# Causal attention with two heads' scores in PSUM: each head's probabilities turned into the banks of its own scores

## The reference, cut to what matters

```python
q_word, k_word, v_word = jnp.split(word_hidden_states @ c_attn_w + c_attn_b, 3, axis=-1)
k = concatenate([k_img, k_word]); v = concatenate([v_img, v_word])     # one image token first
scores = einsum('bhqd,bhkd->bhqk', q, k) / sqrt(8)
scores = where(kj <= qi + 1, scores, -10000.0) + mask
out = einsum('bhqk,bhkd->bhqd', softmax(scores), v)
```

## Time and profile before

| | |
|---|---|
| median of 3 executions | 843.94 us (838.22 to 846.42) |
| profiled execution, its own time | 842.1 us |
| its span in the profile | 839.5 us |
| stage C, from the first score matmul to the last transpose back | 362.8 to 504.4 us of the span |
| PE, DVE, ACT busy over the whole span | 80%, 73%, 62% |

### The profile page before, as it was taken

The page is one execution under the profiler, slowest core; times in us unless marked ns, Lnnn a source line. Parts: engine busy times, 40 slices in busy tenths (PEclk is TensorE's granted clock), DMA queues, the critical chain, the costliest instruction groups (busy, mean ns, idle before and its releaser), DMA issues.

```text
span 839.5 us, 12933 instructions
## 1 busy us (share of the span) xinstructions
PE 670.8 (80%) x4514; PEld 400.6 (48%) x4514; DVE 616.5 (73%) x1349; ACT 520.1 (62%) x1237; POOL 169.6 (20%) x169
## 2 busy tenths in 40 slices
PE   7589976777889889679987878577888695779866
PEld 3222231543556556445555545254656543446545
DVE  7882348468999897777777765999676669986864
ACT  4479977654778778145775764645665475565742
POOL 5030040012889789711000000000000000000000
PEclk8879987887555555956999998879999897899998
DMA  9400000000000000000000000000000000000000
GB/s 300 140 1 1 2 2 0 1 0 1 1 2 1 1 2 1 1 0 1 2 1 1 2 2 0 1 0 1 2 2 1 1 0 1 0 2 1 1 1 25
DMA packets 9059, 10.54 MB, mean 13 GB/s; under 512 B 2746, under 2 KB 7844, under 8 KB 8868
## 3 DMA queue, kind: packets, MB, share of 16 engines
q1 hardware_dynamic: 8996, 9.73, 3.6%
HBM read 9.21 MB, written 0.52 MB: 12 GB/s over the span
## 4 chain that ended last, share of the span: by engine, by line
PE 43%; DVE 36%; ACT 11%; issue 9%; POOL 1%; DMA 0%; ACTq 0%; DVEq 0%; POOLq 0%
PE ps L1390 4%; PE ps L1650 4%; PE ps L1553 4%; DVE s_nmB L1032 3%; DVE s_nmD L1311 3%; PE ps L1633 3%; ACT arena L514 2%; PE ps L1737 2%; PE ps L1540 2%; PE ps L1670 2%; PE ps L1461 2%; PE ps L1745 2%; PE ps L1831 2%; PE ps L1433 2%; PE ps L1812 2%
## 5 line engine op out<-in xcount | busy, mean ns | idle before, releaser
L382 POOL TENSOR_SCALAR arena<-arena,s_rB,s_zpu 128x512 uint8<-128x512 f32 x128 | 115.9, 945 | 42.5 <-DVE s_rB L1005 41.2
L552 ACT ACTIVATE arena<-ps,s_nmB 128x512 f32<-128x512 f32 x128 | 86.6, 683 | 31.8 <-DVE s_nmB L1032 31.2
L574 ACT ACTIVATE arena<-ps,s_nmx 128x512 f32<-128x512 f32 (+3 forms) x128 | 60.7, 527 | 50.2 <-DVE s_nmx L1130 49.7
L1032 DVE TENSOR_REDUCE s_nmB<-ps 128x2 f32<-128x1024 f32 x64 | 77.3, 1217 | 6.9 <-PE ps L1540 6.6
L1125 DVE TENSOR_REDUCE s_nmx<-ps 128x1 f32<-128x512 f32 (+3 forms) x128 | 56.6, 484 | 21.4 <-PE ps L1636 20.9
L514 ACT ACTIVATE arena<-ps 128x1024 f32<-128x1024 f32 x64 | 60.9, 1026 | 6.4 <-PE ps L1445 6.4
L1553 PE MATMUL ps<-cst,arena 128*128 128x128 f32 x256 | 61.0, 417 | 1.7 <-POOL arena L382 0.8
L1396 PE MATMUL ps<-ones 128*128 128x512 f16 x134 | 43.9, 491 | 22.7 <-ACT s_wn L485 6.6
L1540 PE MATMUL ps<-staged 8*128 8x512 f16 x128 | 46.7, 585 | 11.7 <-ACT arena L552 10.9
L1553 PEld LDWEIGHTS ps<-cst,arena 128*128 128x128 f32 x256 | 48.7, 218 | 14.7 <-POOL arena L382 8.2
L1650 PE MATMUL ps<-cst,arena 128*128 128x128 f32 x320 | 46.9, 301 | 8.7 <-issue 5.3
(11 more groups left out here) (344 smaller groups left out, 1515.3 us busy)
## 6 DMA issues: line engine op xcount, KB each, us to landing
vec<-in_vec SPq DMA_DIRECT2D x1, 1882.0 KB, 11.7
w_d<-in_wqkv SPq DMA_DIRECT2D x2, 768.0 KB
vec<-in_vec SPq DMA_DIRECT2D x1, 960.0 KB, 8.2
w_h<-in_w SPq DMA_DIRECT2D x2, 341.0 KB
x_tok<-in_x SPq DMA_DIRECT2D x1, 512.0 KB, 4.1
arena<-in_w_f SPq DMA_DIRECT2D x2, 256.0 KB, 8.0
rope<-in_rope SPq DMA_DIRECT2D x1, 512.0 KB, 10.5
w_do<-in_wo SPq DMA_DIRECT2D x2, 256.0 KB
```

Of the source, the lines that this page charges most:

```text
L382: nc.gpsimd.tensor_scalar(u8[:, n % 4, j // 2, :, 2 * (j % 2)], prob[:, n % 2, j * 512:j * 512 + 512], sm("rB", 8)[:, c:c + 1], sm("zpu", ...
L552: nc.scalar.activation(prob[:, n % 2, j * 512:j * 512 + 512], ps[:, j, :], ACT.Exp, bias=sm("nmB", 8)[:, c:c + 1], accum_out=sm("sumB", 8) ...
L574: nc.scalar.activation(probC[:, n % 2, at(qt):at(qt) + w], ps[:, bank, col:col + w], ACT.Exp, bias=nmx[:, TB * b + qt, h:h + 1]).then_inc( ...
L1032: free(V.tensor_reduce(sm("nmB", 8)[:, c:c + 2], ps[:, 2 * half:2 * half + 2, :], X, ALU.max, negate=True), "maxB")
```

## The change

The separate banks 3 to 5 for the turned probabilities are gone. Head n has its scores in banks 0 to 2 where n is even and in banks 3 to 5 where n is odd (`bank_c`), and its probabilities are turned into the same three banks, once the exponentials of the head have all been taken. Banks 6 and 7 keep their use. With that:

- PE's loop is now: `t_c` of head n; all scores of head n + 2; at odd n `group_c` (the `group_T` of heads n + 3 and n + 4); at n = 4, 8, ... `pv_c`; at n = 6, 10, ... `turn_back`. The scores of head n + 2 wait, bank by bank, for the copies of head n: bank 0 and bank 1 for ACT's, bank 2 for DVE's. `t_c` waits only for the exponentials. The scores of the first two heads are computed ahead of the loop.
- ACT copies the turned banks as two instructions of 512 columns, and they stand between the exponential of tile 3 and those of tiles 2, 0, 1 of the next head. Before, the copy stood behind all four.
- DVE's `stage_c` moves from ahead of the copy L1148 to behind it.
- `ptC` and `ptC_A` count three and two signals per head in place of two and one.

```diff
+        def bank_c(n, bank):
+            return 3 * (n % 2) + bank
...
             for n in range(B * H + 1):
-                b, h = divmod(n, H)
                 if n < B * H:
-                    for i, qt in enumerate((3, 2, 0, 1)):
-                        if i < 2:
-                            act.wait_ge(sem["maxC"], 2 * n + i + 1)
-                        if n >= 2 and i == 0:
-                            act.wait_ge(sem["ptC"], 2 * (n - 1))
...
+                    act.wait_ge(sem["maxC"], 2 * n + 1)
+                    if n >= 2:
+                        act.wait_ge(sem["ptC"], 3 * (n - 1))
+                    exp_c(n, 3)
                 if n >= 1:
                     m = n - 1
-                    act.wait_ge(sem["ptC"], 2 * m + 1)
...
-                    nc.scalar.activation(prob_t(m), ps[:, 3:5, :].rearrange("p a b -> p (a b)"), ACT.Copy).then_inc(sem["ptC_A"], 1)
+                    for i in range(2):
+                        act.wait_ge(sem["ptC"], 3 * m + i + 1)
+                        nc.scalar.activation(prob_t(m)[:, 512 * i:512 * i + 512], ps[:, bank_c(m, i), :], ACT.Copy)\
+                            .then_inc(sem["ptC_A"], 1)
+                if n < B * H:
+                    act.wait_ge(sem["maxC"], 2 * n + 2)
+                    for qt in (2, 0, 1):
+                        exp_c(n, qt)
...
-                    if n % 2 == 0 and n + 2 < B * H:
-                        stage_c(n // 2 + 1)
...
-                    free(V.tensor_copy(prob_v(m), ps[:, 5, 0:256]), "ptC_V")
+                    free(V.tensor_copy(prob_v(m), ps[:, bank_c(m, 2), 0:256]), "ptC_V")
+                if n % 2 == 0 and n + 2 < B * H:
+                    stage_c(n // 2 + 1)
...
-            def s_c(n, parts):
+            def s_c(n, tiles):
...
-                    if n >= 1 and qt:
-                        pe.wait_ge(sem["expC"], 4 * (n - 1) + read)
+                    if n >= 2:
+                        pe.wait_ge(sem["ptC_V" if bank == 2 else "ptC_A"], n - 1 if bank == 2 else 2 * (n - 2) + bank + 1)
...
             def t_c(n):
                 pe.wait_ge(sem["expC"], 4 * n + 4)
-                if n >= 1:
-                    pe.wait_ge(sem["ptC_A"], n)
-                    pe.wait_ge(sem["ptC_V"], n)
...
-                        ins = nc.tensor.transpose(ps[:, 3 + bank, c:c + P], probC[:, n % 2, a:a + P], ident)
-                    if kt in (3, 2):
+                        ins = nc.tensor.transpose(ps[:, bank_c(n, bank), c:c + P], probC[:, n % 2, a:a + P], ident)
+                    if kt != 1:
...
+            group_c(0)
+            for n in range(2):
+                s_c(n, (3,))
+                s_c(n, (2, 0, 1))
+            group_c(1)
+            for n in range(B * H + 3):
                 if n < B * H:
-                    s_c(n, slice(1, 4))
...
+                    t_c(n)
+                if n + 2 < B * H:
+                    s_c(n + 2, (3,))
+                    s_c(n + 2, (2, 0, 1))
+                if n % 2 == 1 and n + 3 < B * H:
+                    if n >= 7 and n % 4 == 3:
+                        pe.wait_ge(sem["oC"], (n - 3) // 4)
+                    group_c((n + 3) // 2)
+                if n >= 4 and n % 4 == 0:
+                    pv_c((n - 4) // 4)
+                if n >= 6 and n % 4 == 2:
+                    g = (n - 6) // 4
                     pe.wait_ge(sem["oT_C"], g + 1)
-                    if n // 2 + 1 <= B * H // 2:
-                        pe.wait_ge(sem["stagedC"], n // 2 + 1)
                     turn_back(7, oT[:, g % 2, :], "toC")
```

More of the change, by code:

```diff
@@ L563, in _, with exp_c @@
             again_c(act, 0, lambda o, a: nc.scalar.activation(o, a, ACT.Copy))
+            def exp_c(n, qt):
+                b, h = divmod(n, H)
+                bank, col = place(qt)
+                w = P * (qt + 1)
+                nc.scalar.activation(probC[:, n % 2, at(qt):at(qt) + w], ps[:, bank_c(n, bank), col:col + w], ACT.Exp,
+                                     bias=nmx[:, TB * b + qt, h:h + 1]).then_inc(sem["expC"], 1)
             for n in range(B * H + 1):
-                b, h = divmod(n, H)
                 if n < B * H:
-                    for i, qt in enumerate((3, 2, 0, 1)):
-                        if i < 2:
-                            act.wait_ge(sem["maxC"], 2 * n + i + 1)
-                        if n >= 2 and i == 0:
-                            act.wait_ge(sem["ptC"], 2 * (n - 1))
[L572 to L575, removed]
+                    act.wait_ge(sem["maxC"], 2 * n + 1)
+                    if n >= 2:
+                        act.wait_ge(sem["ptC"], 3 * (n - 1))
+                    exp_c(n, 3)
                 if n >= 1:
                     m = n - 1
-                    act.wait_ge(sem["ptC"], 2 * m + 1)
                     if m >= 6:
@@ L1124, in _ @@
                             bank, col = place(qt)
-                            ins = V.tensor_reduce(nmx[:, TB * b + qt, h:h + 1], ps[:, bank, col:col + P * (qt + 1)], X,
-                                                  ALU.max, negate=True)
+                            ins = V.tensor_reduce(nmx[:, TB * b + qt, h:h + 1],
+                                                  ps[:, bank_c(n, bank), col:col + P * (qt + 1)], X, ALU.max, negate=True)
                             if qt == tiles[-1]:
@@ L1142, in _ @@
                     m = n - 1
-                    dve.wait_ge(sem["ptC"], 2 * m + 2)
+                    dve.wait_ge(sem["ptC"], 3 * m + 3)
                     if m == 0:
@@ L1626, in s_c @@
                 r = slice(64 * j, 64 * j + 51)
-                for qt, read in ((3, 1), (2, 3), (0, 3), (1, 4))[parts]:
-                    if n >= 1 and qt:
-                        pe.wait_ge(sem["expC"], 4 * (n - 1) + read)
+                for qt in tiles:
                     bank, col = place(qt)
+                    if n >= 2:
+                        pe.wait_ge(sem["ptC_V" if bank == 2 else "ptC_A"], n - 1 if bank == 2 else 2 * (n - 2) + bank + 1)
                     w = P * (qt + 1)
-                    o = ps[:, bank, col:col + w]
-                    M(o, stb[r, G % 2, qt * P:qt * P + P], stb[r, G % 2, 512:512 + w], start=(qt > 0), stop=False)
-                for qt in (3, 2, 0, 1)[parts]:
+                    M(ps[:, bank_c(n, bank), col:col + w], stb[r, G % 2, qt * P:qt * P + P], stb[r, G % 2, 512:512 + w],
+                      start=(qt > 0), stop=False)
+                for qt in tiles:
                     bank, col = place(qt)
-                    ins = M(ps[:, bank, col + P * qt:col + P * qt + P], identb[:, :], cmask[:, :], start=False, stop=(qt != 2))
+                    ins = M(ps[:, bank_c(n, bank), col + P * qt:col + P * qt + P], identb[:, :], cmask[:, :],
+                            start=False, stop=(qt != 2))
                 ins.then_inc(sem["sC"], 1)
@@ L1658, in pv_c @@
                     pe.wait_ge(sem["vC"], b + 1)
-                pe.wait_ge(sem["ptC_A"], 4 * g + 4)
+                pe.wait_ge(sem["ptC_A"], 8 * g + 8)
                 pe.wait_ge(sem["ptC_V"], 4 * g + 4)
@@ L1672, in pv_c, with group_c @@
                 ins.then_inc(sem["pvC"], 1)
-            group_T(0, 7, padqC, padkC, 8, "tC", identb[:, :], psb16)
-            s_c(0, slice(0, 1))
-            for n in range(B * H + 4):
-                if n < B * H:
-                    s_c(n, slice(1, 4))
[L1679 to L1690, removed]
+            def group_c(G):
+                if G == H // 2:
+                    parts_c(1)
+                group_T(G, 7, padqC, padkC, 8, "tC", identb[:, :], psb16)
+            group_c(0)
[4 more added lines that the diff above has]
+            for n in range(B * H + 3):
+                if n < B * H:
+                    t_c(n)
[10 more added lines that the diff above has]
+                    g = (n - 6) // 4
                     pe.wait_ge(sem["oT_C"], g + 1)
-                    if n // 2 + 1 <= B * H // 2:
-                        pe.wait_ge(sem["stagedC"], n // 2 + 1)
                     turn_back(7, oT[:, g % 2, :], "toC")
-                if n >= 5 and n % 4 == 1:
-                    pv_c((n - 5) // 4)
             pe.wait_ge(sem["ocn"], B)
```

## The result

The changed kernel takes 883.12 us (median of 4 executions, 882.13 to 883.53) against 845.18 us for the kernel before on the same chip: a ratio of 1.0453, 95% interval 1.0417 to 1.0488. It is slower by about 38 us. The profiled execution took 882.13 us and its span is 880.3.

A forecast was written before the change was run, and what follows sets the result against it. The prediction took PE, 88% busy in the stage, to set the pace. To 842.1 us it added 26 for waits (six cycles 21, start 5) and 22 for the clock: 890, or 892 on the median, range 862 to 908.

The forecast's parts named there:

- The ring: Stage C: PE's last instruction before the transposes releases, through DVE and ACT, its next scores; PE waits 1.8, 2.4, 1.5 us.
- The three ways round: From group_T through DVE and ACT to PE's scores 3.50 us, with copy L1171 between 4.1, from turn_back 3.2.
- The sum per four heads: Four heads of stage C take 18.8 us against 15.26, 3.5 more; over six cycles +21 us.
- The start of the stage: Ahead of the first pv_c: two more score blocks at clock 0.50 and part of the waits, +5 us, bounds 2.9 and 8.
- The join and the end: Join of the two batches and end of stage C: taken at nothing, bounds -2 and +2 us.
- The clock: Stage C: idle time drops PE's clock to 0.50 in most cycles; 4.4 us in five of seven, +22, bounds none and +34.
- with two pairs 3.8, with three 4.9 us: Cost of a low-clock cycle, by how many pairs of scores and group_T or turn_back (1.15 us each) run slow.
- The swing of the clock: Skill page's rule: cycling through PSUM banks swings the clock; a fall in every cycle, upper bound +34 us, about 902.
- PE was not freed: Rival, 5%: two bank sets give enough slack, PE's 12% of gaps in stage C close, -12 us, 830 to 832.
- The clock did rise in the stage: Rival, 5%, claimed the opposite: the clock never rises in stage C, 80 us more, about 922.
- The rule on repeating gaps: Skill page's rule: gaps repeating on the engine that should be full can mean too few buffers; favoured PE freed, 830 to 832.

The follow-up runs named there:

- e1: The changed kernel with group_c moved ahead of the scores of head n + 2, turn_back left in place; 849.94 us, ratio to before 1.0106.
- e3: The changed kernel with both group_c and turn_back moved ahead of the scores of head n + 2; 843.68 us, ratio to before 0.9981.
- e4: The changed kernel with ACT's two copies of head n ahead of the tile 3 exponential of head n + 1; 862.60 us, ratio to before 1.0228.
- e5: The changed kernel with five thrown-away matmuls of 512 columns behind the transposes at two of four heads; 874.11 us, ratio to before 1.0333.
- e8: e6 with group_c placed ahead of the pv_c halves; 833.22 us, ratio to the kernel before 0.9884.
- e7: The kernel before, one set of score banks, with pv_c cut into halves at two successive heads; 844.96 us, ratio 0.9994.
- e6: e3 with pv_c cut into halves at two successive heads, between transposes and scores; 834.89 us, ratio to the kernel before 0.9915.

## Why the prediction was right, and where it was not

**The ring.** This was the step on which the forecast stood, and it held link by link. The three ways round were worked out as 3.5, 4.1 and 3.2 us; measured are 3.48, 4.08 and 3.23. PE's waits behind the last two, forecast 2.4 and 1.5, are 2.36 and 1.51, and the one forecast at 1.8 is 1.76 where the clock was at 1.00 (scores at 460.82). e1 and e3 show that it is the place of `group_c` and `turn_back` that closes it: with both moved, the whole loss is gone, and banks, waits on banks and copies are the same as in the changed kernel. e4 shows the branch by DVE's own copy.

**The sum per four heads** was 3.5 us; e5 measured 3.7 at a held clock. 18.8 was forecast, 19.00 found.

**The start of the stage** was +5, found +4.8, and in part that is luck. The forecast made it of two more blocks of scores and of waits of the ring. The two longest waits of PE there are others, for DVE's copy of bank 2:

```profile
379.39 0.28 PE L1644 MATMUL ps<-staged 51*128 51x256 bf16 x1 [2.27 <-DVE arena L1158]
...
387.53 0.39 PE L1644 MATMUL ps<-staged 51*128 51x256 bf16 x1 [3.07 <-DVE arena L1158]
```

And the clock, which before stood at 0.50 from 362.8 to 393.6, was 0.60 in the mean between 362.42 and 398.07. The join and the end were taken at nothing: the end gained 0.7, and the join is contained in the next number.

**The clock.** That it would fall in most cycles was right: it fell in each of the six. The size was off. The term was 22 us; from the 36.3 us of the six cycles 22 belong to the ring (6 x 3.7), which leaves 14 for the clock and the join together. The step that failed is "with two pairs 3.8, with three 4.9 us": it assumed two or three pairs of scores and `group_T` at low clock. No cycle had more than one.

In the first cycle the clock fell at about 413.9, when both pairs were over, and only the scores ahead of `pv_c` (418.87 - 416.95 = 1.92, forecast 1.81 at low clock) and a part of `pv_c` (3.25 us to the transposes at 422.12, against 2.3) were long. That is 0.8 + 1.0 = 1.8 us, the number that e5 gave. The slow transposes were hidden in the wait, as forecast: it shrank from some 1.8 to 0.79.

The first two cycles are the cheapest. Over the 19.00 us that e5 found with the clock held, the six cycles took 1.8, 1.8, 3.4, 6.5 (with the join), 3.4 and 2.2 us. In the third the whole `pv_c` was slow (439.69 to 444.12, 4.4 us against 2.3) and one pair ran low in the middle:

```profile
451.55 0.80 PE L1644 MATMUL ps<-staged 51*128 51x384 bf16 x3
452.28 0.50 PE L1648 MATMUL ps<-cmask,identb 128*128 128x128 bf16 x3
452.57 1.06 PE L1480 MATMUL ps<-cst,arena 128*128 128x128 f32 x4
453.43 2.03 PE L1660 MATMUL ps<-cst,arena 128*128 128x128 f32 x10
456.25 0.37 PE L1644 MATMUL ps<-staged 51*128 51x512 bf16 x1 [0.80 <-ACT u L592]
```

Its scores took 1.51 us (451.06 to 452.57) in place of 1.1, and the way round from `turn_back` 3.68 (452.57 to 456.25) in place of 3.23: 0.9 us for the pair, forecast 1.15. The kernel before had also lost time over its own 15.26: 5.3 us in the six cycles, 3.7 of them in the join. So the sum is 19.1 - 5.3 = 13.8, the 14 above. The term was 8 us too large, and that is most of the way from the forecast 892 to the measured 883.

**The swing of the clock.** First the trace: 1.00 and 0.54 by turns in the windows above, mean 0.81. The rule from the Trainium skill, page "TensorE: Matmul & The Clock Gate", section "A second HAM failure mode: psum-queue depth-cycling", by which a kernel that pauses between groups of matmuls swings between the two clock levels, agrees with that in kind. The price it was given here, 34 us, was far too high, for the reason just told. And in e3, which goes through the same banks in the same turns but pauses less, the clock stayed at 1.00 from 396 to 490 in the profiled execution.

**The other rivals.** PE was not freed: it was busy 111.26 of 146.00 us, 76%, not over 88%. The clock did rise in the stage. The rule on repeating gaps (the Trainium skill, page "Perfetto Trace Analysis", section "Identifying Performance Opportunities") was right about the kernel before in one respect only that a later run shows: with the order mended and `pv_c` cut, e8 with the second set of banks is 1.2% faster, and e7, with the cut but one set, is not.

**What stays open.** e8 against e6 (above). And which of the two edits from e3 to e8, the cut or its place, does more was only separated to within the scatter of the runs. The change also moved `stage_c` behind DVE's copy L1158; no run undoes that move alone. For the kernel before, the place of `group_T` did not matter, since nothing behind its copy on DVE was needed by PE's next scores within the same turn; this I argue from the order and have not tried.

## What to carry to other kernels

More buffers lengthen a pipeline only if the in-order queues let it run ahead. After adding them, follow each new wait through all engines back to the instruction that starts it; if that one is the last thing the waiting engine did, the loop is closed, and where it is longer than the work beside it, its length is the period. The cure is then to issue the small producer (here eight transposes for the next pair) as early as its buffer is free, which here gave back 33 of 38 us; and to look at the granted clock, since waits of PE can be paid a second time there.

## What the runs showed of the hardware that was not expected

Extra work made a kernel faster: 60 thrown-away matmuls of 512 columns brought 9 us (883.12 to 874.11), because PE's clock stayed at 1.00 longer (mean 0.91 in place of 0.81). And a fall of the clock to 0.50 cost less than the doubling of the work under it: from 413.90 to 420.70 PE was busy 6.01 of 6.80 us, which is some 3.0 us more than the same work would take at 1.00 (an estimate), and the clock's price was 1.8 us in such a cycle, because the slowed transposes stood where PE would have waited. Where a low stretch took in a whole `pv_c` and another one a pair of scores and `turn_back`, as in the third cycle, the price was 3.4.
